# Four fused cross-attention blocks on one core: expert rows routed by scattered ids, the router's pairs placed in other slots, late rows centred on VectorE, input rows loaded by group

## The chip, the cores and the metric

The kernel runs on one core of one Trainium2 chip. The metric is the device time of one execution in microseconds (us); shown are the median and the range of several executions. The engines are called PE (TensorE, matmuls), DVE (VectorE), ACT (ScalarE), POOL (GpSimd) and SP (SyncE, which here only issues DMAs). "Landing" is the moment at which the last part of a DMA has arrived.

## What is computed

The input x has 16 sequences of 128 rows of width 256 (2,048 rows in all), and so has the context. Four layers follow one another. The first is the one that the change is in:

```python
q = _ln(latents, ...); x = latents + _mha(q, q, ...)        # self-attention, 16 heads of 16
x = x + _mha(_ln(x, ...), _ln(tokens, ...), ...)            # cross-attention
h = _ln(x, moe_ln_g, moe_ln_b)
logits = h @ rw.T + rb                                      # 8 experts
vals, idx = jax.lax.top_k(logits, 2)
gates = jax.nn.softmax(vals, axis=-1)
h1 = gelu(h @ fc1_w[e].T + fc1_b[e])                        # width 1024, each expert e
eo = h1 @ fc2_w[e].T + fc2_b[e]
x = x + (eo[idx] * gates).sum(axis=1)                       # the two chosen experts of each row
```

Then come a layer that picks the 10 best rows of each sequence and lets them attend to the context, a grouped-query attention with a gated feed-forward part, and a last cross-attention with ternary weights. All arithmetic is in fp32.

## The kernel before

The program is a row of blocks; at the end of each (`end_turn`, L231) all engines meet and the semaphores are cleared.

**Constants and first loads** (L274 to L307) are a block of their own: SP loads all of x (2 MB) and the weights of the self-attention, ACT issues eight small loads, POOL writes the constants.

**`attention`** (L517) runs self- and cross-attention as one stream of 32 sequences, t = 0 to 31, in slots; what each engine does in slot t is written out by hand, engine by engine, so the order on each is fixed. Four sequences form a group whose rows are centred on POOL (L898), turned on PE (L629), projected (L636, L645). Each slot then has scores for the row maxima (PE L653, DVE L943), turned scores (PE L663), exponentials (ACT L873), products (PE L673, L678), division (DVE L964) and, for two sequences together, the output rows (PE L688). VP and xn_a are views of the large tile `reg`.

**The router** (class `Router`, L1052) works inside the last slots of that stream, by tables of slots. Rows go in pairs of sequences q = 0 to 7: statistics (DVE L1072, L1075), the deviation (POOL L1080, L1081), centring (POOL L1083), turning (PE L1090), gain and bias (ACT L1096), logits (PE L1104). Sets of sequences k are then ranked and chosen (DVE L1123 to L1137), counted (PE L1148, L1149) and placed (DVE L1154 to L1164): every row gets for each of its two experts a row number in `expert_rows`, a scratch tensor in DRAM of 17,280 rows of 1 KB, which 36 DMAs of SP fill with zeros beforehand (L316). POOL scatters the rows there, one indirect DMA for each sequence and choice, 32 in all (L1177). At the end DVE makes the tables of which expert each of 39 blocks of 128 rows belongs to (L1184 to L1201), and the gates (L1214 to L1224). Where the jobs of PE share a bank of PSUM, the lists `in_a`, `in_b`, `in_c` give their order in the bank.

**The experts' block** takes 39 blocks j = 0 to 38: SP reads 128 rows (`load_rows`, L1044), 1 MB of first weights (`load_up`, L1034) and 1 MB of second weights (`load_down`, L1039) per block into two buffers each, and stores the result over the same rows (`store_rows`, L1049). PE turns the rows (L1289), makes 16 matmuls 128x128 (L1300) and 8 matmuls 128x256 (L1310), each in two passes. SP issues these in this order for j:

```python
sp.wait_ge(M["turned_in"], j + 1); load_rows(sp, j + 2)
sp.wait_ge(M["fc1_full"], FC * (j + 1)); load_up(sp, j + 2)
sp.wait_ge(M["fc2_full"], j); load_down(sp, j + 1)
sp.wait_ge(M["y_ok"], j); store_rows(sp, j - 1)
```

**The next block** collects the results: POOL gathers both expert rows of each sequence (L1457, 32 indirect DMAs), DVE adds them times their gates (`take`, L1733), scores and ranks rows (L1741 to L1771); meanwhile PE projects the context (L1472 to L1490). DVE clears the padded values tok_V first (L1819) and then adds the bias row (L1821), whose bank PE needs next. SP waits for the first gathers and loads the mask and the six weights of the third layer (L323), which POOL scales afterwards (L1463).

## Time and profile before

| | |
|---|---|
| median of 3 runs | 1471.12 us (1466.84 to 1472.11) |
| the profiled execution's own time | 1468.97 us |
| its span, first to last instruction | 1467.2 us |
| PE busy | 1292.2 us (88%) |
| DVE busy | 673.1 us (46%) |
| ACT busy | 621.1 us (42%) |
| POOL busy | 398.9 us (27%) |
| bytes moved by DMA | 139.67 MB |

Busy times are sums over the whole span. The span and the time differ by 1.8 us that lie outside the first and last instruction. In rows of the timeline the first number is the start, the second the duration, both in us; "x4" is the number of instructions merged into the row; in square brackets stands how long the engine had been idle before it and what ended that.

### The profile page before, as it was taken

The page shows a single profiled execution, that of the slowest core. Times are in us where ns is not written, and L with a number is a line of the kernel's source. Part 1 is how long each engine was busy: PE and PEld are TensorE (multiplying, and loading weights), DVE is VectorE, ACT ScalarE, POOL GpSimd, SP SyncE. Part 2 cuts the span into 40 slices and gives each one's busy share as a digit, 9 for nine tenths or more (in the row PEclk, how much of TensorE's full clock was granted, in tenths as well). Part 3 has the DMA queues.
Part 4 walks back from the last instruction along what each step waited for, and adds up shares of the span by engine and source line. Part 5 has one row for each costly group of instructions (what it writes and reads, how often), then busy time and mean ns, then how long its engine had stood idle before and what let it go on. Part 6 is the DMA issues. An engine that isn't in the chain of part 4 may idle for free. (4 is left out here: it accounts for less than half of the span.)

```text
span 1467.2 us, 34284 instructions
## 1 busy us (share of the span) xinstructions
PE 1292.2 (88%) x13938; PEld 1054.0 (72%) x13938; DVE 673.1 (46%) x1410; ACT 621.1 (42%) x1444; POOL 398.9 (27%) x517
## 2 busy tenths in 40 slices
PE   3899999973499999997888569999999999878997
PEld 1566666663489999995576458888888888655665
DVE  3576777784231000003473356455454453336666
ACT  1444445430244444452412036556455564324442
POOL 5224445156000000002640044424334242142200
PEclk9999999996699999998956789999999999989999
DMA  9900000011589999993700000000000000000000
GB/s 352 414 6 2 2 2 2 2 41 61 200 279 330 324 326 330 326 331 122 266 2 2 2 2 1 2 2 1 1 1 2 2 1 1 1 1 2 17 16 30
DMA packets 83324, 139.67 MB, mean 95 GB/s; under 512 B 5344, under 2 KB 63712, under 8 KB 83040
## 3 DMA queue, kind: packets, MB, share of 16 engines
q1 hardware_dynamic: 78816, 128.07, 24.9%
q0 software_dynamic: 3072, 8.39, 1.6%
q8 instruction: 112, 1.84, 0.5%
q10 hardware_dynamic: 1280, 1.01, 0.2%
q14 instruction: 44, 0.36, 0.1%
HBM read 108.36 MB, written 29.10 MB: 94 GB/s over the span
## 5 line engine op out<-in xcount | busy, mean ns | idle before, releaser
L1344 ACT ACTIVATE w_ca<-scores,fc1b 128x128 f32<-128x128 f32 x312 | 113.7, 367 | 139.6 <-PE scores L1300 119.7
L873 ACT ACTIVATE reg<-scores 128x1024 f32<-128x1024 f32 x96 | 93.0, 1021 | 143.6 <-PE scores L663 143.2
L1300 PEld LDWEIGHTS scores<-reg 128*128 128x128 f32 x1248 | 148.1, 195 | 4.5 <-issue 2.6
L1300 PE MATMUL scores<-reg 128*128 128x128 f32 x1248 | 148.6, 278 | 2.1 <-issue 1.1
L943 DVE TENSOR_REDUCE reg<-scores 128x8 f32<-128x1024 f32 x96 | 113.0, 1219 | 63.0 <-PE scores L653 63.0
L1310 PE MATMUL bank<-reg,w_ca 128*128 128x256 f32 x624 | 141.1, 379 | 0.3 <-DVE small L1358 0.3
L2042 ACT ACTIVATE reg<-reg,mx 128x128 f32<-128x128 f32 x256 | 99.2, 389 | 83.8 <-DVE mx L2222 83.5
L1367 DVE TENSOR_TENSOR reg<-bank,reg 128x256 f32<-128x256 f32 x39 | 16.6, 425 | 240.8 <-PE bank L1310 228.5
L1310 PEld LDWEIGHTS bank<-reg,w_ca 128*128 128x128 f32 x624 | 115.5, 190 | 14.6 <-DVE small L1358 0.3
L2131 POOL TENSOR_TENSOR reg<-reg,rden 128x512 f32<-128x512 f32 x64 | 66.5, 1040 | 210.8 <-DVE rden L2227 210.7
L1958 PE MATMUL scores<-reg 128*128 128x128 f32 x1024 | 122.4, 279 | 0.5 <-ACT reg L2065 0.5
L1958 PEld LDWEIGHTS scores<-reg 128*128 128x128 f32 x1024 | 119.7, 196 | 0.7 <-ACT reg L2065 0.7
L1951 PE MATMUL bank<-reg 128*128 128x256 f32 x512 | 118.8, 385 | 0.8 <-issue 0.8
L1457 POOL DMA_INDIRECT reg<-expert_rows,pick_row x32 | 30.7, 958 | 326.5 <-issue 320.4
L1951 PEld LDWEIGHTS bank<-reg 128*128 128x128 f32 x512 | 94.7, 190 | 26.6 <-issue 13.2
L964 DVE RECIPROCAL reg<-bank 128x256 f32<-128x256 f32 x48 | 84.2, 1754 | 31.9 <-PE bank L678 30.9
L820 ACT ACTIVATE reg<-bank,qk_bias,shape_c 128x512 f32<-128x512 f32 x96 | 69.5, 778 | 56.4 <-PE bank L636 56.0
L1958 PE MATMUL bank<-reg 128*128 128x128 f32 x640 | 78.4, 279 | 0.7 <-ACT reg L2072 0.7
L1958 PEld LDWEIGHTS bank<-reg 128*128 128x128 f32 x640 | 76.7, 195 | 1.9 <-ACT reg L2072 1.1
L2249 DVE TENSOR_TENSOR reg<-scores,reg 128x512 f32<-128x512 f32 x32 | 22.1, 692 | 109.8 <-PE scores L1958 109.8
L653 PEld LDWEIGHTS scores<-reg 32*128 32x128 f32 x1536 | 48.7, 190 | 28.1 <-ACT reg L873 22.9
L663 PEld LDWEIGHTS scores<-reg 32*128 32x128 f32 x1536 | 47.5, 186 | 25.1 <-issue 25.0
(258 smaller groups left out, 2283.3 us busy)
## 6 DMA issues: line engine op xcount, KB each, us to landing
reg<-in_fc SPq DMA_DIRECT2D x78, 1024.0 KB, 7.5
expert_rows<-reg SPq DMA_DIRECT2D x36, 480.0 KB, 14.7
reg<-expert_rows SPq DMA_DIRECT2D x39, 128.0 KB, 5.9
expert_rows<-reg SPq DMA_DIRECT2D x39, 128.0 KB, 6.8
xres<-in_x SPq DMA_DIRECT2D x1, 2048.0 KB, 11.4
ctxr<-in_ctx SPq DMA_DIRECT2D x1, 2048.0 KB, 8.2
w_l<-in_w_l SPq DMA_DIRECT2D x2, 1024.0 KB, 11.8
out<-xres SPq DMA_DIRECT2D x8, 256.0 KB, 2.7
```

The lines of the kernel that those rows point to most:

```text
L653: ins = nc.tensor.matmul(S[r][:, (2 * s + c) * P:(2 * s + c + 1) * P], Qs[rows_of(r), (b // GB) % 2, s, c, batch(b)], Ks[rows_of(r), (b // ...
L820: ins = nc.scalar.activation(dst[:, g % 2, s, m, :], bank[:, :], ACT.Identity, scale=scale[:, s:s + 1], bias=bias[:, s, m:m + 1])
L873: ins = nc.scalar.activation(PT2[:, t % 2, 2 * half:2 * half + 2, :, :, :].rearrange("p r s c q -> p (r s c q)"), scores4[:, 2 * half:2 * ...
L943: ins = nc.vector.tensor_reduce(mxpad.rearrange("p (c n d) -> p n c d", c=C, d=DH)[:, 4 * half:4 * half + 4, :, 0], scores4[:, 2 * half:2 ...
L964: link(nc.vector.reciprocal(rd, banks[4][:, 2 * P:4 * P]))
L1300: ins = nc.tensor.matmul(S[n % 4][:, 0:P], up_w8[j % 2][:, c, f * P:(f + 1) * P], xbT[:, j % 2, c, :], start=(c == 0), stop=(c == C - 1))
L1310: ins = nc.tensor.matmul(T[j % 2][:, 0:D], h1[:, j % 2, f, :], down_w8[j % 2][:, f, :], start=(f == 0), stop=(f == FC - 1))
L1344: nc.scalar.activation(h1[:, j % 2, f, :], S[n % 4][:, 0:P], ACT.Gelu, bias=fc1b[:, bass.ds(e * FC + f, 1)]).then_inc(M["fc1_free"], 1)
L1951: ins = nc.tensor.matmul(bank[:, 0:D], src[:, f, :], w[:, f, :], start=(f == 0), stop=(f == FC - 1))
L1958: ins = nc.tensor.matmul(bank[:, k * P:(k + 1) * P], w[:, c, w0:w0 + P], src[:, c, :], start=(c == 0), stop=(c == C - 1))
L2042: ins = nc.scalar.activation(v[:, a, :], v[:, a, :], ACT.Exp, bias=cols_of(mx, n)[:, a:a + 1], accum_out=cols_of(psum, n)[:, a:a + 1])
L2131: nc.gpsimd.tensor_tensor(v, v, spread(rden, n), ALU.mult).then_inc(M["scaled"], 1)
```

## The change

It has these parts.

- **Routing by ids.** The rows no longer travel. The centred rows are stored once, pair by pair, as `routed_rows` (`store_routed`, SP). POOL scatters for each row and choice only two int32 numbers, the row's own number and the number of its result row, into `sorted_ids`, which nine DMAs fill with padding ids beforehand in place of the 36 DMAs of zeros. In the experts' block SP loads the 128 id pairs of a block four blocks ahead (`load_ids`), POOL gathers the rows by the first id (`gather_rows`) and scatters the results by the second into `expert_out` (`scatter_rows`), where both results of a row lie side by side. The next block reads them with 16 plain DMAs on SP (`expert_rows_in`), instead of 32 gathers on POOL.
- **Slots.** The router's first pairs are turned and ranked two slots sooner, in seven sets instead of five. From slot 27 (`LATE`) on, the router's jobs stand behind the attention's on PE, ACT and DVE.
- **Late rows on DVE.** Pairs 5 to 7 are centred on DVE; POOL only makes the deviations (`late_rstd`).
- **Rows by group.** The first block is gone; its work stands at the head of `attention`. x is loaded in four DMAs, one per group, and the first group is centred on DVE.
- **Weights.** Five of the six weights of the third layer are loaded among the experts' blocks (`grouped_at`). Of the experts' first weights, only one block's goes out before the ids are there.
- **The rest.** The gates are finished in the experts' block; POOL clears tok_V, in three parts.

```diff
+        id_dram = nc.dram_tensor("sorted_ids", (SROWS, 2), mybir.dt.int32, kind="Internal").ap()
+        xn_dram = nc.dram_tensor("routed_rows", (B * P, D), F32, kind="Internal").ap()
+        ys_dram = nc.dram_tensor("expert_out", (YROWS, D), F32, kind="Internal").ap()
...
-        ZEROS = 36
-        ZN = SROWS * D // P // ZEROS
...
-        zeros = view(17408, [ZN])
...
-                sp.dma_start(xres[:], A["x"].rearrange("b p d -> p b d")).then_inc(ld["x"], 16)
...
-        end_turn()
...
+        def first_rows(sp):
+
+            for g in range(G):
+                sp.dma_start(xres[:, g * GB:(g + 1) * GB, :], A["x"].rearrange("b p d -> p b d")[:, g * GB:(g + 1) * GB, :])\
+                    .then_inc(ld_x[g], 16)
+                if g == 0:
+                    sp.dma_start(w_sa[:], A["w_sa"].rearrange("(c p) n -> p c n", p=P)).then_inc(ld["sa"], 16)
...
-            for k in range(ZEROS):
-                sp.dma_start(xs_dram.rearrange("(p r) d -> p (r d)", p=P)[:, k * ZN:(k + 1) * ZN], zeros)\
-                    .then_inc(ld["zeros"], 16)
+            sp.wait_ge(M["ids_ok"], 1)
+            for a in range(ID_PARTS):
+                sp.dma_start(id_dram[a * P * ID_ROWS:(a + 1) * P * ID_ROWS, :].rearrange("(p r) d -> p (r d)", p=P),
+                             padding_ids[:, :, :].rearrange("p r d -> p (r d)")).then_inc(ld["ids"], 16)
             sp.dma_start(down_bias, A["fc2b"]).then_inc(ld["fc2b"], 16)
...
+        def store_routed(sp, q):
+
+            sp.wait_ge(M["rows_ok"], 2 * q + 2)
+            sp.dma_start(xn_dram.rearrange("(b p) d -> p b d", p=P)[:, 2 * q:2 * q + 2, :], routed[:, 2 * q:2 * q + 2, :])\
+                .then_inc(ld["xn"], 16)
...
-                    in_c.append(("y", pair_out(t)))
+                    (in_c if router is None or t < LATE else in_b).append(("y", pair_out(t)))
+                if t >= LATE:
+                    turns = [("rx", q) for q in routed("turn", t)]
+                    results = [("re", t)] if has_results(t) else []
+                    in_c += results + turns if t < N + 1 else turns + results
...
+                        if t < LATE:
+                            routed_turns(t)
+                            routed_results(t)
...
+                        if LATE <= t < N + 1:
+                            routed_results(t)
+                            routed_turns(t)
+                        if t >= N + 1:
+                            routed_turns(t)
+                            routed_results(t)
...
-                                pool.wait_ge(ld["zeros"], 16 * ZEROS)
+                            if g == 0:
+                                pool.sem_inc(M["rstd_ok"], 1)
+                                continue
...
-                            router.centre(pool, link, q)
+                            if q < router.ON_VECTOR:
+                                router.centre(pool, nc.gpsimd, link, q)
+                            elif q + 1 < B // 2:
+                                router.late_rstd(pool, link, q)
+                        if router is not None and t + 1 == router.slots["stats"][-1]:
+                            router.late_rstd(pool, link, B // 2 - 1)
                         for k in routed_sets("place", t):
                             router.scatter(pool, k)
                     if router is not None:
-                        pool.wait_ge(M["scattered"], 16 * 2 * B)
+                        pool.wait_ge(ld["xn"], 16 * B // 2)
+                        gather_rows(pool, 0)
+                        gather_rows(pool, 1)
...
+                            dve.wait_ge(M["rstd_ok"], 1)
+                            for j in range(GB):
+                                nc.vector.tensor_scalar(xn_a[:, j, :], xres[:, j, :], mv[:, 0, j, 0:1], rstd[:, 0, j:j + 1],
+                                                        ALU.subtract, ALU.mult).then_inc(M["hx_ok"], 1)
                             nc.vector.memset(mxpad, 0.0)
-                            nc.vector.memset(VP[:, :, :, :, :], 0.0).then_inc(M["pad_ok"], 1)
+                            nc.vector.memset(VP[:, 0, :, :, :], 0.0).then_inc(M["pad_ok"], 1)
+                            nc.vector.memset(VP[:, 1, :, :, :], 0.0).then_inc(M["pad_ok"], 1)
...
+                            if q >= router.ON_VECTOR:
+                                router.centre(dve, nc.vector, link, q)
+                        if t >= LATE:
+                            take_results(t)
...
+        def load_ids(sp, j):
 
             r = sp.value_load(block_row[0:1, j:j + 1], min_val=0, max_val=SROWS - P)
-            sp.dma_start(xb[:, j % 2, :], xs_dram[bass.ds(r, P), :]).then_inc(rows_in[j % 2], 16)
-
-        def store_rows(sp, j):
-
-            r = sp.value_load(block_row[0:1, j:j + 1], min_val=0, max_val=SROWS - P)
-            sp.dma_start(ys_dram[bass.ds(r, P), :], yb[:, j % 2, :]).then_inc(y_stored[j % 2], 16)
+            sp.dma_start(block_ids_of[:, j, :], id_dram[bass.ds(r, P), :]).then_inc(ids_in[j % 4], 16)
+
+        def gather_rows(pool, j):
+
+            pool.wait_ge(ids_in[j % 4], 16 * (j // 4 + 1))
+            if j >= 2:
+                pool.wait_ge(M["turned_in"], j - 1)
+            nc.gpsimd.indirect_dma_start(xb[:, j % 2, :], None, xn_dram,
+                                         bass.IndirectOffsetOnAxis(block_ids_of[:, j, 0:1], 0)).then_inc(rows_in[j % 2], 16)
+
+        def scatter_rows(pool, j):
+
+            pool.wait_ge(M["y_ok"], j + 1)
+            if j >= 1:
+                pool.wait_ge(y_stored[(j - 1) % 2], 16 * ((j - 1) // 2 + 1))
+            nc.gpsimd.indirect_dma_start(ys_dram, bass.IndirectOffsetOnAxis(block_ids_of[:, j, 1:2], 0),
+                                         yb[:, j % 2, :], None).then_inc(y_stored[j % 2], 16)
...
-                "turn": [23, 24, 25, 27, 29, 31, 33, 35],
-                "logits": [26, 26, 28, 28, 32, 32, 34, 36],
+                "turn": [22, 23, 25, 27, 29, 31, 33, 35],
+                "logits": [24, 24, 26, 28, 30, 32, 34, 36],
             }
 
-            sets = [(0, 4), (4, 4), (8, 4), (12, 2), (14, 2)]
+            sets = [(0, 4), (4, 2), (6, 2), (8, 2), (10, 2), (12, 2), (14, 2)]
             set_slots = {
-                "rank": [26, 28, 32, 34, 36],
-                "choose": [27, 29, 32, 34, 36],
-                "count": [28, 30, 33, 35, 37],
-                "place": [28, 30, 33, 35, 37],
+                "rank": [24, 26, 28, 30, 32, 34, 36],
+                "choose": [25, 26, 28, 30, 32, 34, 36],
+                "count": [26, 27, 29, 31, 33, 35, 37],
+                "place": [26, 27, 29, 31, 33, 35, 37],
             }
+
+            ON_VECTOR = 5
...
+            def late_rstd(self, pool, link, q):
+                self.deviations(pool, link, q)
+                pool.sem_inc(M["late_rstd"], 1)
+
+            def centre(self, eng, ops, link, q):
+                if q < self.ON_VECTOR:
+                    self.deviations(eng, link, q)
+                else:
+                    eng.wait_ge(M["late_rstd"], q - self.ON_VECTOR + 1)
...
-                        nc.gpsimd.indirect_dma_start(xs_dram, bass.IndirectOffsetOnAxis(pick_row[:, s, b:b + 1], 0),
-                                                     routed[:, b, :], None).then_inc(M["scattered"], 16)
+                        nc.gpsimd.indirect_dma_start(id_dram, bass.IndirectOffsetOnAxis(pick_row[:, s, b:b + 1], 0),
+                                                     token_ids[:, b, s, :], None).then_inc(M["scattered"], 16)
...
-                    load_up(sp, j)
-                    load_down(sp, j)
+                load_up(sp, 0)
                 sp.wait_ge(M["tables"], 2)
                 sp.wait_ge(M["scattered"], 16 * 2 * B)
-                for j in range(2):
-                    load_rows(sp, j)
+                for j in range(4):
+                    load_ids(sp, j)
+                load_up(sp, 1)
...
+        grouped_at = {8: "wkv2", 13: "wo2", 18: "wg2", 23: "wu2", 28: "wd2"}
...
-                        load_rows(sp, j + 2)
+                        if j + 4 < NBLK:
+                            load_ids(sp, j + 4)
                         sp.wait_ge(M["fc1_full"], FC * (j + 1))
                         load_up(sp, j + 2)
-                    if j >= 1:
-                        if j + 1 < NBLK:
-                            sp.wait_ge(M["fc2_full"], j)
-                            load_down(sp, j + 1)
-                        sp.wait_ge(M["y_ok"], j)
-                        store_rows(sp, j - 1)
+                    if j >= 1 and j + 1 < NBLK:
+                        sp.wait_ge(M["fc2_full"], j)
+                        load_down(sp, j + 1)
+                    if j in grouped_at:
+                        load_grouped(sp, grouped_at[j])
...
+                for j in range(NBLK):
+                    if j + 2 < NBLK:
+                        gather_rows(pool, j + 2)
+                    if j >= 2:
+                        scatter_rows(pool, j - 2)
+                scatter_rows(pool, NBLK - 2)
+                scatter_rows(pool, NBLK - 1)
...
+                def expert_rows_in(g):
+                    if g >= 2:
+                        sp.wait_ge(M["taken"], 2 * GB * (g - 1))
+                    for j in range(GB):
+                        b = g * GB + j
+                        sp.dma_start(picked[:, g % 2, j, :, :].rearrange("p k d -> p (k d)"),
+                                     ys_dram[2 * P * b:2 * P * (b + 1), :].rearrange("(p k) d -> p (k d)", k=2))\
+                            .then_inc(ld_pick[b], 16)
...
-                            nc.gpsimd.indirect_dma_start(picked[:, g % 2, j, k, :], None, ys_dram,
-                                                         bass.IndirectOffsetOnAxis(pick_row[:, k, g * GB + j:g * GB + j + 1], 0))\
-                                .then_inc(ld_pick[g * GB + j], 16)
+                for k in range(3):
+                    nc.gpsimd.memset(tok_V[:, k, :, :, :], 0.0).then_inc(M["pad_ok"], 1)
...
-                nc.vector.memset(tok_V[:, :, :, :, :], 0.0).then_inc(M["pad_ok"], 1)
```

How the order moves is shown at three places. The first is DVE at the start of the program, before:

```order
L928 BN_STATS st<-xres 128x6
L933 BN_AGGR mv<-st 128x2
L989 TENSOR_SCALAR reg<-ones,cols 128x128 x2
...
L995 TENSOR_SCALAR qk_bias<-cols,shape_c 128x2
L997 MEMSET reg 128x256
L998 MEMSET reg 128x4096
L1000 TENSOR_TENSOR route<-bank,rows 128x256
```

and in the change:

```order
L1056 TENSOR_SCALAR reg<-ones,cols 128x128 x2
...
L1062 TENSOR_SCALAR qk_bias<-cols,shape_c 128x2
L1066 TENSOR_SCALAR reg<-xres,mv,rstd 128x256 x4
L1068 MEMSET reg 128x256
L1069 MEMSET reg 128x2048
L1070 MEMSET reg 128x2048
L1072 CAST padding_ids<-shape_c 128x30
L1074 CAST token_ids<-shape_c 128x64
L1077 TENSOR_TENSOR route<-bank,rows 128x256
```

The first group's centring (L1066) has come to DVE, ahead of the clearing of VP (`reg`), which is in two halves; POOL no longer does it.

The second is PE in slots 31 to 34. L663 (now L687) are the turned scores of the last sequence, L673 and L678 (L697, L702) its products, L688 (L712) output rows, L1090 (L1198) turns a pair for the router, L1104 (L1212) makes logits, L1148 and L1149 (L1256, L1257) count. Before:

```order
L1090 MATMUL bank<-ident,reg 128x128 x4
L663 MATMUL scores<-reg 128x128 x16
L688 MATMUL bank<-w_ca,reg 128x256 x4
L673 MATMUL bank<-reg 32x128 x16
L678 MATMUL bank<-reg,ones_half 32x256 x8
L1104 MATMUL bank<-rw,reg 128x8 x8
L1090 MATMUL bank<-ident,reg 128x128 x4
L1148 MATMUL bank<-w_sa 128x32
L1149 MATMUL bank<-w_sa,ones 128x32
L688 MATMUL bank<-w_ca,reg 128x256 x4
```

and in the change:

```order
L687 MATMUL scores<-reg 128x128 x16
L712 MATMUL bank<-w_ca,reg 128x256 x4
L1256 MATMUL bank<-w_sa 128x16
L1257 MATMUL bank<-w_sa,ones 128x16
L1198 MATMUL bank<-ident,reg 128x128 x4
L697 MATMUL bank<-reg 32x128 x16
L702 MATMUL bank<-reg,ones_half 32x256 x8
L1212 MATMUL bank<-rw,reg 128x8 x4
L712 MATMUL bank<-w_ca,reg 128x256 x4
L1198 MATMUL bank<-ident,reg 128x128 x4
```

The turning of a pair no longer stands ahead of the turned scores or of the last output rows.

The third is POOL in the router's last slots. L1080 and L1081 (now L1178, L1179) make the deviation, L1083 (L1191) centres two sequences, L1177 (L1286) are the scatters. Before:

```order
L1083 TENSOR_SCALAR reg<-xres,small 128x256 x2
L1177 DMA expert_rows<-reg,pick_row 17280x256 x8
L1080 TENSOR_SCALAR small<-small 128x2
L1081 TENSOR_TENSOR small<-small,nhalf 128x2
L1083 TENSOR_SCALAR reg<-xres,small 128x256 x2
L1177 DMA expert_rows<-reg,pick_row 17280x256 x8
```

and in the change:

```order
L1286 DMA sorted_ids<-token_ids,pick_row 17280x2 x4
L1178 TENSOR_SCALAR small<-small 128x2
L1179 TENSOR_TENSOR small<-small,nhalf 128x2
L1178 TENSOR_SCALAR small<-small 128x2
L1179 TENSOR_TENSOR small<-small,nhalf 128x2
L1286 DMA sorted_ids<-token_ids,pick_row 17280x2 x12
L1136 DMA reg<-routed_rows,block_ids_of 128x256 x2
```

The centring of the late pairs is gone from POOL, both last deviations stand ahead of the last twelve scatters, and the first two gathers of rows (L1136) stand behind them in the same block.

## Rows read from the trace of the kernel before

**Rows 1.** Busy time by stretch, all engines: experts' blocks, and the block after them
```profile
core 0: us, PE busy (x) PEld busy (x) DVE busy (x) ACT busy (x) POOL busy (x), PEclk, DMA share, GB/s
...
450.00:700.00 250.00, 239.01 (x1587) 220.44 (x1587) 27.18 (x63) 115.56 (x315) 13.44 (x14) 0.97 0.88 296
...
710.00:720.00 10.00, 7.85 (x38) 5.06 (x37) 8.40 (x38) 2.47 (x5) 3.03 (x4) 0.84 1.02 399
```

**Rows 2.** Timeline of the start: ACT's last small load, DVE, POOL, PE
```profile
4.20 0.56 ACTq L290 DMA_DIRECT2D rw<-in_rw  x1
...
15.39 0.45 DVE L989 TENSOR_SCALAR reg<-ones,cols 128x128 f32<-128x128 f32 x2
...
17.03 4.90 POOL L898 TENSOR_SCALAR reg<-xres,mv,rstd 128x256 f32<-128x256 f32 x4
...
17.66 0.27 DVE L997 MEMSET reg<- 128x256 f32 x1
...
21.99 1.97 PE L629 MATMUL bank<-ident,reg 128*128 128x128 f32 x8 [3.96 <-POOL reg L898]
```

**Rows 3.** DMA issues by line: queue, count, KB each, median us from issue to landing
```profile
reg<-in_fc SPq DMA_DIRECT2D x78, 1024.0 KB, 7.5
...
expert_rows<-reg,pick_row POOLq DMA_INDIRECT x32, 2.4
reg<-expert_rows,pick_row POOLq DMA_INDIRECT x32, 3.7
...
rw<-in_rw ACTq DMA_DIRECT2D x1, 8.0 KB, 7.7
```

**Rows 4.** Timeline of slots 31 and 32: PE turning a pair, last turned scores, last division
```profile
325.41 0.63 PE L1090 MATMUL bank<-ident,reg 128*128 128x128 f32 x4 [3.02 <-POOL reg L1083]
...
325.97 1.17 PE L663 MATMUL scores<-reg 32*128 32x128 f32 x32
...
331.21 1.76 DVE L964 RECIPROCAL reg<-bank 128x256 f32<-128x256 f32 x1 [1.34 <-PE bank L678]
```

**Rows 5.** Timeline of the router's last pairs: DVE, POOL and PE
```profile
346.08 0.74 DVE L1072 BATCH_NORM_STATS2 small<-xres 128x6 f32<-128x256 f32 x2
...
353.57 0.73 POOL L1081 TENSOR_TENSOR small<-small,nhalf 128x2 f32<-128x2 f32 x1
...
356.98 1.09 PE L1090 MATMUL bank<-ident,reg 128*128 128x128 f32 x4 [11.03 <-POOL reg L1083]
...
361.43 0.29 DVE L1123 TENSOR_TENSOR w_sa<-w_sa 128x128 f32<-128x128 f32 x1
...
363.31 0.37 DVE L1137 TENSOR_TENSOR w_sa<-w_sa 128x8 f32<-128x8 f32 x2
...
366.18 0.17 DVE L1164 CAST pick_row<-w_sa 128x2 int32<-128x2 f32 x1
```

**Rows 6.** Timeline from the last scatters to the experts' first turn
```profile
370.41 0.96 POOL L1177 DMA_INDIRECT expert_rows<-reg,pick_row  x1 [0.30 <-issue]
...
377.38 1.47 SPq L1044 DMA_DIRECT2D reg<-expert_rows  x2
...
382.85 2.46 DVE L1355 TENSOR_REDUCE small<-w_l 128x1 f32<-128x512 f32 x4 [8.57 <-PEq L231]
...
385.01 0.69 PE L1289 MATMUL bank<-ident,reg 128*128 128x128 f32 x2 [19.76 <-DMA reg<-expert_rows]
```

**Rows 7.** Timeline of two experts' blocks: PE's first matmuls of each
```profile
659.04 3.73 PE L1300 MATMUL scores<-reg 128*128 128x128 f32 x32
...
666.29 3.73 PE L1300 MATMUL scores<-reg 128*128 128x128 f32 x32
```

**Rows 8.** Timeline of the two blocks after the experts: DVE, PE
```profile
684.53 5.18 DVE L1819 MEMSET reg<- 128x6144 f32 x1 [1.23 <-issue]
...
690.04 1.11 PE L1472 MATMUL bank<-ident,ctxr 128*128 128x128 f32 x4 [4.61 <-DVE route L1821]
...
847.23 0.35 DVE L2196 TENSOR_SCALAR reg<-xres,rstd 128x256 f32<-128x256 f32 x1 [1.68 <-POOL rstd L2125]
```

230 lines of the change are left out of this document (131 added, 99 removed).

## The prediction

> **What bounds the kernel now.** I read the busy time by stretch first. PE is busy for 239 of 250 us among the experts and DMA is then busy for 0.88 of the time [rows 1], so there the matmuls set the pace, with DMA close behind. The change touches that stretch little; what it can win lies at three places where PE stands still, which the timeline shows.
>
> At the start PE turns its first rows at 21.99 us, and had waited 3.96 us for POOL's centring [rows 2]. At the end of the router it waits for POOL three times: 3.02 us at 325.41 [rows 4] and 11.03 us at 356.98 [rows 5] are two of them. POOL spends 0.96 us on each indirect DMA and 0.30 between two [rows 6], so 32 of them take 40 us of the engine that must also centre the late pairs. Then comes the longest gap, 19.76 us until the experts' first rows land, PE starting at 385.01 [rows 6]. The third place is small: at 690.04 PE has waited 4.61 us for DVE's bias row, which stands behind a memset of 5.18 us [rows 8].
>
> **The start.** Today the statistics and the bias columns end at 17.93 (17.66 + 0.27, with the memset), 2.3 us after the bias columns begin at 15.39, and POOL centres from 17.03 for 4.90 us [rows 2]. In the change DVE needs a quarter of x, then the small loads, the last of which is asked for at 4.20 [rows 2] and landed 7.7 us later [rows 3], at 11.9. That load competes with the same megabytes of x and weights as before, so I leave it there. Bias columns to 14.2; then DVE centres, four times 0.35 us [rows 8], to 15.6 with the gaps; PE turns at 15.9. 21.99 less 15.9 is **6.1 us** won. It cannot be more than 10 (the meeting of the engines that is gone ends at about 13 us, the loads remain), and if x in four parts delays the small loads it may be 3. DVE's memset of VP now stands behind the centring, its statistics for group 1 come at about the same time as PE's work moves forward, and POOL has lost 4.9 us of centring, so I cost that at nothing. The 36 DMAs of zeros go; nobody waits for them in the rows, so they are worth nothing.
>
> **The last slots of attention.** Call T the start of the last turned scores, 325.97 today [rows 4]. The 3.02 us ahead of it [rows 4] go, since no turning stands before the turned scores any more. Against that, DVE, whose maxima and divisions lie in each slot's chain, gets more there: ranking and choosing a set of two took 361.43 to 363.68, 2.25 us [rows 5], and now comes in slots 26, 28 and 30 too, the first time beside a set of four's places; in slot 30 DVE also waits for POOL's deviation (0.73 us, [rows 5]) and centres (0.7). How much of it is hidden no row shows; between 0 and 8 us, I take 3, since a slot has room on DVE after its subtraction. The two cancel: **0**.
>
> **The tail.** DVE ends the last division at T + 7.0 (331.21 + 1.76, [rows 4]). Then it works in rounds: statistics 0.74 [rows 5], a wait for POOL's 0.73, centring 0.7, ranking and choosing 2.25, and with about 1 us for small operations and gaps that is 5.4 us; then counting on PE and placing, 363.68 to 366.35, 2.7 us [rows 5]. Two such rounds of 8.1 us, and a last one of 2.25 + 2.7 and 0.6 for the gates' first half: T + 29. POOL has sent the earlier sets by then (its last deviation is at about T + 18, the eight scatters before the last four take 10 us), so the last four start at T + 29.5, the last of them at 33.5, and it lands 2.4 us later [rows 3], at T + 36. SP then issues four loads of ids and one of weights. Two issues took 1.47 us with 0.35 for the second's own [rows 6], so 1.12 each, 5.6 in all: T + 42. The meeting of the engines cost 4.0 us (378.85 to 382.85, [rows 6]): T + 46. The gathered rows are there: ids at 36 + 1 + 2.4, gather 0.96 to issue and 3.7 to land [rows 3] is T + 44. PE starts at T + 46.5, where today it starts at 385.01, T + 59.0 [rows 6]. **12.5 us** won. No row prices a load of 8 bytes per partition; between 2.4 and 7.5 us [rows 3] I take 2.4, as it has hardly any bytes and no weights before it but one block's.
>
> **The experts.** PE's period is 7.25 us (659.04 to 666.29, [rows 7]). A block moves 2.36 MB, which is 325 GB/s. POOL now issues one gather and one scatter per block, 2.5 us of the 7.25, and each has a whole block to land. Row loads stay 128 KB. The new demand is 4.7 MB of the third layer's weights in blocks 8 to 28. One such load is about 3 us of DMA; a weight load lands 7.5 us after issue [rows 3] and is needed 10 us after it (two periods less one 3.73 us of matmuls [rows 7], less the issue), so one more megabyte just fits and must be worked off in five blocks: 5 times 2.36 plus 1.05 MB in 36.2 us, 355 GB/s. DMA has moved 399 GB/s at 710 us [rows 1]. I take **2 us** lost, between 0 and 12 (4.7 MB at 399 GB/s, nothing hidden). The Trainium skill, *DMA: Bandwidth & Descriptors*, section Bandwidth, has 341 GB/s for transfers of 1 MB; by it the 31 blocks from 8 on, 77.9 MB, would take 228.4 us instead of 224.6, and 3.8 us would be lost in place of 2. The trace speaks against it as a ceiling by the 399 just named.
>
> **After the experts.** The last store is an indirect DMA, issued in 0.96 us and landing in 2.4 like those of [rows 3], where SP's took about a microsecond less: 1 us lost. DVE's memset of 5.18 us [rows 8] goes to POOL, and PE's bank comes free 5 us sooner. POOL's scaling of weights now starts sooner, when DVE ranks the first rows for PE; how much it slows DVE no row shows, between 0 and the 5 us just won; I take 1.5. Together **2.5 us** won. The 32 gathers that go from POOL were not waited for by PE.
>
> **The sum.** 6.1 + 0 + 12.5 - 2 + 2.5 = 19.1 us. From the profiled execution's own time, 1468.97, that is 1449.9. It lies 2.15 us below the median of the runs, 1471.12, so the changed kernel's median may lie at 1449.9 to 1452.1; I say 1451.
>
> **The rivals.**
> *More is won.* DVE's added work in the slots is hidden wholly (3 more), the small loads land sooner with x behind them (3 more), no DMA waits (2), the scaling hurts nobody (1.5), and the experts' first blocks run without the waits that SP's long list brought: 1440. For it: SP no longer stands behind results. Against it: four things must go well together.
> *DVE becomes the bound.* In the last slots it centres, waits for POOL and ranks; 5 us more before T (8 in place of 3) and 2 us more in each of the rounds, since each wait for POOL can fall behind a scatter of 1.26 us: 10 us less won, 1461. For it: DVE then carries statistics, centring, ranks and places in one queue. Against it: it idled for most of the tail before.
> *The start gives nothing.* x by group does not do what it says, if the small loads behind it on the same DMA engines set the start: 1457.
> *Slower: DMA becomes the bound among the experts.* The gathers and scatters, with ids in 8-byte pieces and the added weights, make the blocks wait. The price is 39 times what a block gains in length. From 0.5 us per block on, all that is won is gone; at 0.72 it is 28 us lost, 1479. A block would then have 7.97 us for its 2.36 MB and 0.12 MB of added weights, 311 GB/s. For it: DMA is busy for 0.88 of the stretch already, and the part may be higher where no block waits. Against it: 399 GB/s in the stretch in which POOL's gathers and the same weights ran together [rows 1].
>
> **How the numbers follow.** The forecast 0.54, more 0.17, DVE 0.17, the start 0.06, DMA 0.06. The forecast's own range, from the bounds above, is 1443 to 1459. The range for 8 in 10 reaches to both middle rivals: 1436 to 1464. A difference of 0.5%, 7.4 us, is about what can be told from none. Faster than 1463.8: nearly all of the forecast, all of the first and third rival and two thirds of the second, 0.86. Slower than 1478.5: 0.05. Between: 0.09.
>
> **What would show it.** In the new profile PE's first turning should start near 16 us; the last turned scores near 320; the first turn among the experts near 366; the wait of PE for POOL's centring should be gone, and DVE busy from division to last place with waits for POOL of a microsecond. Among the experts the period should stay 7.25 us, with gaps of under a microsecond behind blocks 8, 13, 18, 23 and 28. The prediction is wrong in its main part if PE's first expert turn comes less than 8 us sooner after T than 59 us, and wrong in its sign only if the period grows.

## The result, and the profile after

The change is worth almost nothing where it was first compared. The kernel before took 1471.41 us (median of 20 runs, 1466.84 to 1473.22), the changed one 1467.66 us (20 runs, 1462.45 to 1472.35); the ratio is 0.9982, 95% interval 0.9974 to 0.999. That is faster by 2.6 us by the ratio (3.75 by the medians), where 20 were forecast, and 1467.66 lies outside the range of 1436 to 1464.

The experiments ran on other chips, and there the same two kernels differ by much more: 1503.2 us before (9 runs), 1481.5 after (5 runs), ratio 0.9855, interval 0.9834 to 0.9876. They were four chips, numbers 10, 4, 1 and 9; on each of them the kernel before has a median of 1501.0 to 1503.2 us, and below they are called "the later chips". (The expectations, written at the time, say "the second chip" for all four.) The number of the first comparison's chip is not known; it is "the first chip" here. Nothing is compared across the two kinds unless it is said.

The two profiled executions of the first chip, laid side by side (each moment is the start of an instruction that both kernels have; "lead" is by how much the changed kernel is ahead):

| moment | before | after | lead | step |
|---|---|---|---|---|
| PE turns the first rows | 21.99 | 16.91 | 5.1 | +5.1 |
| turned scores of slot 20 | 225.33 | 220.08 | 5.3 | +0.2 |
| last turned scores, T | 325.97 | 329.38 | -3.4 | **-8.7** |
| experts' first turn on PE | 385.01 | 388.13 | -3.1 | +0.3 |
| DVE's last bias of the experts | 677.71 | 680.43 | -2.7 | +0.4 |
| first DVE operation of the next block | 681.91 | 690.98 | -9.1 | **-6.4** |
| first of the third layer | 844.52 | 845.86 | -1.3 | **+7.7** |
| first of the last layer | 1297.54 | 1298.94 | -1.4 | -0.1 |
| end of the span | 1467.2 | 1465.5 | 1.7 | **+3.1** |

So the gain was not absent: 16.8 us were won in six steps and 15.2 given back in three. The rows behind the table follow, from the timeline of the changed kernel (columns as in the rows of before). The start, which answers to [rows 2]:

```profile
4.65 0.46 ACTq L303 DMA_DIRECT2D rw<-in_rw  x1
...
13.40 0.48 DVE L1056 TENSOR_SCALAR reg<-ones,cols 128x128 f32<-128x128 f32 x2 [6.02 <-DMA rw<-in_rw]
...
15.47 1.38 DVE L1066 TENSOR_SCALAR reg<-xres,mv,rstd 128x256 f32<-128x256 f32 x4
...
16.91 1.97 PE L653 MATMUL bank<-ident,reg 128*128 128x128 f32 x8 [0.83 <-DVE reg L1066]
```

DVE waits for the last small load to 13.40, centres in 1.38, and PE turns at 16.91. Slot 22, where the lead of 5.3 us begins to go:

```profile
243.15 0.63 PE L1198 MATMUL bank<-ident,reg 128*128 128x128 f32 x4 [2.92 <-POOL reg L1191]
243.71 2.09 PE L687 MATMUL scores<-reg 32*128 32x128 f32 x32
```

The first pair is turned one slot sooner than before, ahead of the turned scores of slot 22, and POOL has not centred it: PE waits 2.92 us, and after the wait the 32 matmuls take 2.09 us instead of 1.17. PE's granted clock, as a share of the full 2.4 GHz, is 0.62 from 243 to 246 us, a mean of its two levels 1.2 and 2.4 GHz; before the wait it was 1.0. (The list of the change says that the first pairs are turned two slots sooner; it is one slot for the turning and two for the ranking.) Before the change, the turned scores of this slot came 10.05 us behind those of slot 21; now 13.6. By the turned scores of slot 24 the changed kernel has lost 6.3 us (42.4 us from slot 20 against 36.1). The turned scores of slots 27 and 28, and what follows them:

```profile
293.98 1.26 PE L687 MATMUL scores<-reg 32*128 32x128 f32 x32 [3.37 <-DVE reg L1012]
...
303.91 1.17 PE L687 MATMUL scores<-reg 32*128 32x128 f32 x32 [0.77 <-DVE reg L1012]
...
308.90 1.94 ACT L919 ACTIVATE reg<-scores 128x1024 f32<-128x1024 f32 x2 [7.68 <-remote]
308.95 0.87 DVE L1044 SCALAR_TENSOR_TENSOR reg<-bank,shape_c,reg 128x256 f32<-128x256 f32 x2 [2.47 <-remote]
310.89 1.45 PE L677 MATMUL scores<-reg 32*128 32x128 f32 x20 [4.65 <-ACT reg L919]
```

At 293.98, in slot 27, PE waits for DVE's maxima, which stand behind the places of one set and the ranks of the next. At 308.9 two engines wake together from a wait that no instruction of the trace ends ("remote"): the scores they wait for are marked as done at 305.1. No run isolates this one gap; the experiments show gaps of its kind on the later chips. The tail, with the last division, DVE's last place, the first weight load, the last scatter, SP's loads of ids, the second gather and PE's first turn among the experts, which answer to [rows 5, 6]:

```profile
339.47 1.76 DVE L1033 RECIPROCAL reg<-bank 128x256 f32<-128x256 f32 x1 [2.34 <-PE bank L702]
...
363.51 0.17 DVE L1272 CAST pick_row<-w_sa 128x2 int32<-128x2 f32 x1
...
367.56 0.40 SPq L1119 DMA_DIRECT2D reg<-in_fc  x1
...
367.74 0.96 POOL L1286 DMA_INDIRECT sorted_ids<-token_ids,pick_row  x1 [0.30 <-issue]
...
376.01 3.68 SPq L1129 DMA_DIRECT2D block_ids_of<-sorted_ids  x4
...
380.14 0.97 POOL L1136 DMA_INDIRECT reg<-routed_rows,block_ids_of  x1 [0.30 <-issue]
...
388.13 0.66 PE L1400 MATMUL bank<-ident,reg 128*128 128x128 f32 x2 [25.03 <-PEq L245]
```

Eight us lie between the last scatter and SP's answer, and another seven between the second gather and the end of the meeting. What the meeting holds is seen by its own line (columns: duration in ns min/median/max, first and last start), at 381 and at 684 us, and, in the kernel before, at 379 us:

```profile
L245 POOLq DRAIN  x1: 6022/6022/6022, 381.3 to 381.3; - x1
...
L245 POOLq DRAIN  x1: 6257/6257/6257, 683.9 to 683.9; - x1
```

```profile
L231 POOLq DRAIN  x1: 2678/2678/2678, 379.3 to 379.3; - x1
```

POOL does not meet the others before its drain is over. After the experts it costs 6.26 us that the kernel before did not have. The experts themselves went as forecast (period 7.24 us, 661.41 to 668.65), in answer to [rows 1, 7]:

```profile
450.00:700.00 250.00, 234.16 (x1578) 218.20 (x1577) 22.32 (x52) 113.18 (x310) 64.77 (x64) 0.97 0.92 318
...
661.41 3.73 PE L1411 MATMUL scores<-reg 128*128 128x128 f32 x32
...
668.65 3.73 PE L1411 MATMUL scores<-reg 128*128 128x128 f32 x32
```

And the block after them, in answer to [rows 8], and the last layer:

```profile
690.94 5.48 POOL L1582 MEMSET reg<- 128x2048 f32 x3 [8.85 <-POOLq L245]
690.98 1.91 DVE L1934 TENSOR_SCALAR reg<-ones,cols 128x128 f32<-128x128 f32 x2 [10.13 <-PEq L245]
...
694.87 1.92 PE L1595 MATMUL bank<-ident,ctxr 128*128 128x128 f32 x8
...
1302.64 1.38 DVE L1066 TENSOR_SCALAR reg<-xres,mv,rstd 128x256 f32<-128x256 f32 x4 [0.46 <-POOLq L946]
...
1304.07 1.67 PE L653 MATMUL bank<-ident,reg 128*128 128x128 f32 x8 [0.54 <-DVE reg L1066]
```

PE's wait of 4.61 us for the bias row is gone (context rows turned at 694.87, 3.9 us behind DVE's start instead of 8.1). The last layer's attention also has its first group centred on DVE: its first turning comes 5.1 us after its first statistics, 8.6 before.

### The profile page after: what moved, and what is told of

It is laid out like the page before. It is cut to its first block and busy times, and to the rows that moved or that the text cites. A ratio compares the mean times of both kernels' runs of the same rounds, so it can differ in the third digit from the quotient of the medians.

```text
span 1465.5 us, 34213 instructions
## 1 busy us (share of the span) xinstructions
PE 1293.6 (88%) x13946; PEld 1057.4 (72%) x13946; DVE 677.2 (46%) x1457; ACT 621.7 (42%) x1444; POOL 431.4 (29%) x551
## 5 line engine op out<-in xcount | busy, mean ns | idle before, releaser
L1421 PEld LDWEIGHTS bank<-reg,w_ca 128*128 128x128 f32 x624 | 115.9, 191 | 14.2 <-DVE small L1476 0.3
L1144 POOL DMA_INDIRECT expert_out<-reg,block_ids_of x39 | 38.7, 992 | 153.1 <-DVE reg L1485 96.6
L687 PEld LDWEIGHTS scores<-reg 32*128 32x128 f32 x1536 | 48.5, 190 | 28.7 <-issue 28.7
## 6 DMA issues: line engine op xcount, KB each, us to landing
ctxr<-in_ctx SPq DMA_DIRECT2D x1, 2048.0 KB, 15.2
```

The source lines that it names most:

```text
L1421: ins = nc.tensor.matmul(T[j % 2][:, 0:D], h1[:, j % 2, f, :], down_w8[j % 2][:, f, :], start=(f == 0), stop=(f == FC - 1))
```

## The experiments

All ran on the later chips. Two things must be known to read them. The changed kernel itself ran on chips 10 and 4 only, so the ratio to the kernel before, which ran on each of the four, compares better than the medians do. And executions of one kernel there differ by 3.3 to 3.7 us already before the router begins (in the changed kernel and its variants slot 20's turned scores start at 216.1 to 216.9, or at 219.6 to 221.2), where PE's granted clock dips in slots 1 and 10 or does not. So beside the medians I give three distances from the profiled executions: slot 20 to T, T to the experts' first turn, and their sum. While scatters run in the slots, a single profile leaves some 4 us open in the first of these: the edit of the late first weights lies behind T, and yet it has 123.9, where three other profiles whose edits lie behind T or that have none show 119.5 to 120.0.

| kernel | chip | median us | ratio to before | 20 to T | T to experts | sum |
|---|---|---|---|---|---|---|
| before | all | 1501.0 to 1503.2 | | 108.0 | 63.5 | 171.5 |
| changed | 10 | 1481.5 | 0.9855 | 120.0 | 58.4 | 178.4 |
| changed, again | 4 | 1477.8 | 0.9844 | 120.0 | 58.2 | 178.2 |
| drains among the experts | 1 | 1473.5 | 0.9819 | 119.5 | 58.6 | 178.0 |
| first weights late | 1 | 1476.3 | 0.9828 | 123.9 | 55.1 | 179.0 |
| first pairs turned in slot 23, 24 | 1 | 1476.2 | 0.9828 | 120.0 | 58.9 | 178.9 |
| old slot tables | 1 | 1475.5 | 0.9831 | 105.9 | 69.3 | 175.2 |
| ids in rows of 64 bytes | 10 | 1472.5 | 0.9809 | 119.0 | 56.3 | 175.3 |
| late pairs centred on POOL | 4 | 1478.8 | 0.9849 | 118.1 | 62.6 | 180.7 |
| scatters held back | 4 | 1489.5 | 0.9931 | 109.5 | 83.1 | 192.6 |

On the first chip the sums are 159.7 before and 168.1 after (100.6 + 59.0, 109.3 + 58.8).

**Both kernels on later chips.** No edit; both ran on chip 10, the changed one again on chip 4.

> The changed kernel itself, beside the others on their chip, since the four experiments before showed the kernel before 30 us slower (1501) than in the first comparison, and themselves at 1474 to 1476. Theory 'stutter': while POOL scatters pieces of 8 bytes, PE waits in its own queue (gaps of 0.3 to 1.5 us between single matmuls that wait for no semaphore) and a 16 KB packet of instructions takes 2 to 3.4 us instead of at most 1.5; this differs from chip to chip, so T (the last turned scores) will lie anywhere from 329 to 344 and the time follows it. Rival: the experiments' own edits caused it; then T is 329 here too.

> The kernel before with a profile, on the chip of the others. If this chip is one that makes the kernel before slow (1501), the profile shows where; theory: not in the slots (T within 2 us of 326, its scatters are of 1 KB pieces) but among the experts, where 1 KB scattered rows and the loads share the DMA engines, or in the wait for the scatters. If it is a chip like the first, 1467 to 1473.

> The changed kernel once more, beside the next three, since the chip decides much: 1467.7 on the first, 1481.5 on the second. On the second chip I expect 1480 to 1483, T (last turned scores) at 338 to 341, PE's first turn among the experts at 398 to 399; on a chip like the first 1467 and 329.

Measured: 1481.53 us (1477.88 to 1486.06) and 1477.84 (1476.93 to 1479.09) for the changed kernel, T at 340.2 and 336.5; 1500.97 for the one before, T at 334.4. I had expected the kernel before to be disturbed among the experts and not in the slots. It is the other way round: from the first turn among the experts to the last it has 275.8 us, and 277.7 on the first chip. But slots 29 and 30 (from the turned scores of each to the next) have 14.2 and 8.9 us instead of 7.0 and 8.8, and the block after the experts 182.1 us instead of 162.6. There PE stands still with no semaphore to wait for while POOL issues its 32 gathers. The timeline of the kernel before on chip 10, PE:

```profile
713.79 0.66 PE L1472 MATMUL bank<-ident,ctxr 128*128 128x128 f32 x4 [1.26 <-issue]
727.10 1.12 PE L1472 MATMUL bank<-ident,ctxr 128*128 128x128 f32 x4 [12.64 <-issue]
```

The changed kernel has no indirect DMA in that block, and there it has 157.3 us on chip 10 (159.3 on chip 4, 154.9 on the first chip). This is why the change is worth 22 us on chip 10 and 3 on the first: 24.8 us against 7.7 in this one block. That the gathers alone do it there is not shown: during the wait of 12.64 us weights of the third layer are being loaded too (DMA moves 408 GB/s from 714 to 727.5 us), and five of these loads have also left the block with the change. In the slots, its scatters of ids do to PE what the scatters of rows did; the timeline of PE in slot 28, changed kernel, chip 10:

```profile
303.24 0.29 PE L697 MATMUL bank<-reg 128*32 128x128 f32 x1 [0.45 <-issue]
303.95 0.27 PE L697 MATMUL bank<-reg 128*32 128x128 f32 x1 [0.42 <-issue]
304.67 0.40 PE L697 MATMUL bank<-reg 128*32 128x128 f32 x3 [0.45 <-issue]
306.08 0.65 PE L697 MATMUL bank<-reg 128*32 128x128 f32 x3 [1.01 <-issue]
```

32 matmuls that take 1.08 us in other slots are spread over 7 us, one or a few at a time.

**Scatters held back.** None of POOL's scatters runs beside slots 26 to 32.

```diff
-                        for k in routed_sets("place", t):
-                            router.scatter(pool, k)
+                        if router is not None and t >= 33:
+                            for k in (range(5) if t == 33 else routed_sets("place", t)):
+                                router.scatter(pool, k)
```

> All scatters of ids of the first five sets are held back to slot 33, so that none runs while the attention's slots 26 to 32 do. Theory 'stutter': PE's gaps that wait for no semaphore come from POOL's indirect DMAs beside it; without them T lies 100 to 106 us behind slot 20's turned scores (108.0 in the kernel before and 119.9 in the changed one on the second chip), so T at 320 to 326 and slots 28 to 31 at 8 to 10 us each; the 20 scatters then take 25 us behind T and PE's first turn comes at T + 66 to 70, so the time falls by 2 to 8 on the second chip and is the same or worse on the first. Rival 'DVE': slots 27 to 31 are long because DVE ranks and centres there; T stays within 3 us of the changed kernel's and the time rises by 9.

Measured: 1489.46 us (1487.0 to 1496.99), where I had expected it to fall by 2 to 8. From slot 20 to T 109.5 us instead of 120.0 on the same chip, which is the first chip's 109.3, though not the 100 to 106 that I expected. The waits of PE from 260 to 345 us (us in total, times, longest), changed kernel on chip 10:

```profile
PE scores L687 <- DVE reg L1012: 3.9, 2, 3.4
PE bank L697 <- issue: 3.7, 7, 1.0
...
PE scores L677 <- issue: 1.7, 1, 1.7
PE scores L687 <- issue: 0.9, 1, 0.9
```

and with the scatters held back, where no wait of PE is left that ends on "issue":

```profile
PE scores L687 <- DVE reg L1013: 8.0, 4, 3.4
PE bank L1199 <- DVE w_sa L1263: 2.2, 3, 1.7
```

So the stutter in the slots, single matmuls some tenths of a microsecond apart with no semaphore to wait for, comes from POOL's indirect DMAs: that is shown. It also shows that the 8.7 us which the first chip lost before T do not need the stutter: with none, the distance is the same 109.5. The waits for DVE's maxima, 8.0 us, remain: DVE's ranking and placing in the slots' chain. That the held-back version is slower was to be had from the rows of before: 20 scatters of 1.26 us now stand one after another on POOL, and the tail grows by all of their 25 us, not by the 8 to 12 that my T + 66 to 70 allowed.

**The first pairs turned one slot later.**

```diff
-                "turn": [22, 23, 25, 27, 29, 31, 33, 35],
-                "logits": [24, 24, 26, 28, 30, 32, 34, 36],
+                "turn": [23, 24, 25, 27, 29, 31, 33, 35],
+                "logits": [25, 25, 26, 28, 30, 32, 34, 36],
...
-                "rank": [24, 26, 28, 30, 32, 34, 36],
+                "rank": [25, 26, 28, 30, 32, 34, 36],
```

> The first two pairs are turned in slots 23 and 24 (as before the change), their logits made and ranked in slot 25. Theory 'early turn': PE's wait of 2.92 us for POOL's centring in slot 22, and the half clock that follows it, go; the turned scores of slot 22 start at 240.2 instead of 243.7 and those of slot 31 at about 325 instead of 329.4; the time falls by 3 to 5 us. Rival 'moved': DVE's ranking of four sequences now stands in slot 25 beside the subtraction there and the slots after it lose what was won; T stays at 328 to 330 and the time does not move.

Measured: 1476.16 us (1471.45 to 1478.46). The timeline of PE in slots 22 and 23:

```profile
240.53 1.17 PE L687 MATMUL scores<-reg 32*128 32x128 f32 x32
...
247.91 0.60 PE L1198 MATMUL bank<-ident,reg 128*128 128x128 f32 x4
248.44 1.17 PE L687 MATMUL scores<-reg 32*128 32x128 f32 x32
```

The wait and the fallen clock are gone, and at slot 24 the kernel is 6.3 us ahead of the changed one (36.1 us from slot 20 against 42.4). Slot 25, with the ranking of four sequences, takes 3.1 back, and by T nothing is left that could be told (120.0). The first theory holds for its slot, the rival for the sum, as long as the scatters run in the slots; without them it is otherwise, as the variants at the end show.

**Old slot tables,** in all else the changed kernel (the tables and the five sets as before the change, shown in the diff above).

> All slot tables and the five sets as before the change, the rest of the change kept (late jobs behind the attention's, late pairs centred on DVE, ids). Theory 'slots cost': the last turned scores start at 320 to 323 instead of 329.4, as seven sets put ranking and choosing into more slots' chains; but the larger sets 8 to 11 are ranked in slot 32 and lengthen the tail by 2 to 4 us; the time falls by 3 to 6. Rival 'LATE and DVE': the delay of slots 27 to 31 comes from the order from slot 27 on and DVE's centring, and stays with the old tables; T at 325 or more and the time within 2 us of the changed kernel.

Measured: 1475.49 us (1471.63 to 1478.87). T comes 14 us sooner (105.9 from slot 20 against 120.0), more than I expected, and the tail takes 10.9 of it back (69.3 against 58.4). The new tables (earlier turning, seven sets), then, buy 11 us behind T and pay 14 ahead of it. The order from slot 27 on and the centring on DVE are not what delays T: they are in this kernel too, and it has 2.1 us less than the kernel before (108.0).

**Late pairs centred on POOL.**

```diff
-            ON_VECTOR = 5
+            ON_VECTOR = 8
...
-                        if router is not None and t + 1 == router.slots["stats"][-1]:
-                            router.late_rstd(pool, link, B // 2 - 1)
```

> All pairs are centred on POOL again (only this part undone). Theory: centring on DVE is worth its place in the tail, where each of the last rounds waits for it: POOL's centring of a pair takes 2.4 us against 0.74, so two rounds grow by 1.7 us each, and a centring that falls behind four scatters waits 5 us more; T loses or wins at most 1, PE's first turn at T + 62 to 68 instead of T + 58.6, the time 3 to 8 us more. Rival: DVE's load in the slots is what delays T; then T falls by 3 or more and the time is the same or lower.

Measured: 1478.8 us (1476.35 to 1482.91), the sum of distances 180.7 against 178.2 on the same chip: the tail 4.4 us longer, T 1.9 sooner. By the distances, centring on DVE is worth 2.5 us, less than the 12.5 of the tail that I had put on it and the order together; the medians, 1478.8 and 1477.84, do not tell the two apart, where 3 to 8 us had been expected.

**The first weight load behind the loads of ids.**

```diff
-                load_up(sp, 0)
                 sp.wait_ge(M["tables"], 2)
                 sp.wait_ge(M["scattered"], 16 * 2 * B)
                 for j in range(4):
                     load_ids(sp, j)
+                load_up(sp, 0)
                 load_up(sp, 1)
```

> The experts' first weight load goes behind the loads of ids instead of ahead of the wait for the scatters. Theory 'queue': the last scatter landed 7.7 us after its issue began because the megabyte of weights was in the same DMA engines ahead of it; it now lands after 2.4, SP loads the ids 4 to 5 us sooner, and PE's first turn among the experts comes 3 to 4.5 us sooner (388.1 to 384.5 or so); the time falls by 3 to 4. Rival 'small writes': scatters of 8 bytes are slow by themselves at the end of a run of 12; nothing moves, or PE starts later by up to 3 us, as the weights now land last.

**Ids in rows of 64 bytes.** `sorted_ids` has 16 numbers in a row instead of two; a scatter writes 64 bytes, the loads still read the first two.

```diff
+IDW = 16
...
-        id_dram = nc.dram_tensor("sorted_ids", (SROWS, 2), mybir.dt.int32, kind="Internal").ap()
+        id_dram = nc.dram_tensor("sorted_ids", (SROWS, IDW), mybir.dt.int32, kind="Internal").ap()
...
-                                                     token_ids[:, b, s, :], None)
+                                                     token_flat[:, 4 * b + 2 * s:4 * b + 2 * s + IDW], None)
```

> The id table's rows are widened from 8 to 64 bytes, so each scatter writes 128 pieces of 64 bytes (what follows the ids in a row is never read). Theory 'small pieces': writes of 8 bytes are served slower than they come and pile up in DRAM, which delays their landing (to 7 us and more) and the fetching of instructions; with 64 bytes a scatter lands after 2.4 us, no instruction packet takes over 1.5 us in slots 26 to 37, T comes to 318 to 323, SP's loads of ids follow the last scatter by 3 to 4 us, and the time is 8 to 15 us below the changed kernel beside it. Rival 'pieces count': it is the number of pieces (128 per DMA, one DMA each 1.26 us), whatever their size; then T and the landing stay as in the changed kernel and the time is the same within 2 us. The padding's nine DMAs carry 1.1 MB instead of 0.14 early in the program; I expect nothing from that.

Measured: first weights late 1476.33 us (1472.39 to 1478.03), wide ids 1472.47 (1470.65 to 1476.19). The wide ids are 9.1 us below the changed kernel on the same chip by the medians; the sum of distances has 3.1 of it, and 3.4 lie ahead of slot 20 (216.83 against 220.22), where the edit does nothing. The stutter hardly cares about the size: 119.0 us from slot 20 to T, where 318 to 323 for T itself was forecast and 335.8 came, so the rival holds there. But between the start of the last scatter and SP's first load of ids, a wait that is the landing alone, both edits act, and they add up (the lower row is of kernels described below, which differ in more):

| | 8 bytes | 64 bytes |
|---|---|---|
| weight load ahead | 8.45 (378.05 to 386.50) | 5.79 (373.83 to 379.62) |
| weight load behind | 5.33 (375.35 to 380.68) | 3.16 (370.95 to 374.11) |

With the weight load moved and nothing else the wait is 5.59 us (381.78 to 387.37), against 8.27 to 9.03 in the three profiles of the changed kernel. So the megabyte ahead or beside costs 2.6 to 3.1 us, the small pieces 2.2 to 2.7 with twelve scatters in a row. With all 32 in a row and no megabyte in flight the pieces cost more: 7.81 us with 8 bytes (394.00 to 401.81, scatters held back) and 3.16 with 64 (384.55 to 387.71, the first of the variants at the end). Scatters of 8 bytes are slow by themselves, then, and the more so the more of them run together, as the rival of the moved weight load had it; both theories hold in part. The Trainium skill, *DMA: Bandwidth & Descriptors*, section Queues, rings and completion order, says that the write which reports a DMA as done lands only after all earlier writes of its DMA engine, across its queues; a load issued on SP's queue ahead of POOL's last scatter then holds the scatter's report back. The upper row fits this; that the scatter's pieces themselves stand behind the megabyte would give the same times, and no run separates the two. The same page, section Specifications, puts the size below which a DMA engine reads, changes and writes back at 512 bytes; 8 and 64 bytes lie both below it and yet differ by 2 us and more here, so that rule alone does not explain the second effect.

**Drains among the experts.**

```diff
                     if j >= 2:
                         scatter_rows(pool, j - 2)
+                    if j % 6 == 5:
+                        nc.gpsimd.drain()
```

> POOL's DRAIN ahead of the meeting of the engines took 6.26 us after the experts (76 indirect DMAs issued since the last one), though the last scatter had landed; before the change it took 2.68 us in the block with 32 scatters and 2.66 in the one with 32 gathers. Theory 'count': a drain costs 0.083 us for each indirect DMA issued since the last drain. A drain every six blocks among the experts then leaves some 6 for the last: it takes about 0.5 us, the block ends 5.5 us sooner, the time falls by 5 to 6 us, and each early drain takes about 1 us in POOL's idle time. Rival 'landing': the drain waits for the last transfers' completion, whatever their number; the last one stays at 6 us and the time does not move. Second rival: the early drains hold the gathers up and PE waits for rows; the experts' stretch grows by some us.

Measured: 1473.51 us (1472.66 to 1475.17). The last drain:

```profile
L245 POOLq DRAIN  x1: 537/537/537, 693.4 to 693.4; - x1
```

From PE's last turn among the experts to the clearing of the semaphores there are 19.5 us, and 25.2 in the changed kernel: 5.7 won, as forecast. The changed kernel was not run on this chip; the ratios to the kernel before, 0.9819 against 0.9855 and 0.9844, fit with intervals that overlap. A drain costs 6.257 us for 76 indirect DMAs, 2.678 and 2.661 for 32, 0.537 for 6: 0.082 to 0.090 us each, and all nine profiles with 76 show 6.257. A drain with none costs 0.04. Wrong was the price of the early ones: 6 to 8 us each, not 1; transfers are in flight at each of them, and the drain seems to wait for these. POOL had the time; the experts' stretch is 277.0 us, against 278.2 and 275.0 in the two profiles of the changed kernel on later chips.

**A version that beats both.** Wide ids, the first pairs turned in slots 23 and 24, drains every six blocks and behind two sets of scatters, the first weights behind the ids and the second in the experts' block.

```diff
                         for k in routed_sets("place", t):
                             router.scatter(pool, k)
+                            if k in (2, 3):
+                                nc.gpsimd.drain()
...
-                load_up(sp, 0)
                 sp.wait_ge(M["tables"], 2)
                 sp.wait_ge(M["scattered"], 16 * 2 * B)
                 for j in range(4):
                     load_ids(sp, j)
-                load_up(sp, 1)
+                load_up(sp, 0)
...
                 load_down(sp, 0)
+                load_up(sp, 1)
                 load_down(sp, 1)
```

> Wide ids as in the kernel beside it, the first two pairs turned in slots 23 and 24, drains of POOL every six blocks and after two sets of scatters, and the first weight load behind the loads of ids, the second in the next block. Theory: the causes add up: against the kernel with wide ids alone 5.5 us from the last drain, 3 to 5 from the slots, 2 to 4 from the gap ahead of the experts: 11 to 14 us less. PE's first turn comes at T + 48 to 52. Rival: the gap ahead of the experts is set by the landing of the gathers in any order, and only 8 us are won.

> The wide version once more, to stand beside the other two on one chip: 1457 to 1461 on the second chip, 1445 to 1452 if the chip is like the first.

Measured: 1459.05 us (1456.31 to 1463.49), ratio to the kernel before 0.9718, interval 0.97 to 0.9735; the second time 1463.67 (1458.95 to 1467.0), 0.9742, interval 0.9721 to 0.9762. The first is 22.5 us below the changed kernel on the same chip, and 13.4 below the wide ids alone, as forecast (11 to 14); the second, on chip 9, is 14 to 18 us below the changed kernel's two medians and misses its own forecast of 1457 to 1461. Its sums are 165.6 and 166.7, with PE's first turn at T + 50.4 and T + 50.6, as the last scatter is seen after 3.16 us and the drain is short. The two drains between the scatters took 7.0 and 6.4 us of POOL each. The meeting ahead of the experts, gather, drain and first turn:

```profile
374.11 3.73 SPq L1135 DMA_DIRECT2D block_ids_of<-sorted_ids  x4
376.50 1.00 POOL L1142 DMA_INDIRECT reg<-routed_rows,block_ids_of  x1 [4.59 <-DMA block_ids_of<-sorted_ids]
...
382.24 0.66 PE L1408 MATMUL bank<-ident,reg 128*128 128x128 f32 x2 [15.93 <-PEq L247]
```

```profile
L247 POOLq DRAIN  x1: 1973/1973/1973, 379.4 to 379.4; - x1
```

It was not run on the first chip, so that it beats both there is an inference and not shown: what it removes (5.7 us of drain after the experts, some 8 of the gap ahead of them) is in the first chip's profile too.

**Variants of it.** With the scatters held back instead of the drains between them; with 8-byte ids; with 8-byte ids and the early pairs in two sets of four. The edit of the last:

```diff
-            sets = [(0, 4), (4, 2), (6, 2), (8, 2), (10, 2), (12, 2), (14, 2)]
+            sets = [(0, 4), (4, 4), (8, 2), (10, 2), (12, 2), (14, 2)]
...
-                "place": [26, 27, 29, 31, 33, 35, 37],
+                "place": [28, 30, 31, 33, 35, 37],
```

> The version that beat both (1459 on the second chip), but with the scatters held back to slot 33 instead of drains between them. Theory: T falls by 8 to 12 (no stutter), the tail grows by 8 to 10 and POOL's drain before the meeting of the engines is 2.8 us instead of 2.0; the time is within 4 us of 1459. Rival: the held scatters also delay the last ones beyond POOL's free time, and it is 5 to 10 us slower than 1459.

> The version that took 1459 on the second chip, with the id table back at 8 bytes a row. Rival 'pieces count' (the size of the pieces is nothing): the time is within 3 us of the wide version beside it, PE's gaps without a semaphore in slots 26 to 32 are 5 to 8 us in both. Theory 'small pieces': 4 to 8 us slower than the wide one, scatters land later, and SP's loads of ids follow the last scatter by 5 us or more in place of 3.2.

> 8-byte ids and everything else of the best version, but the early pairs in two sets of four as before the change (slots 26 to 30), the later ones in twos. Theory: T lay 105.9 us behind slot 20 with the old tables and 115.2 with seven sets, of which ranking in slots 24 to 28 has 3 to 5; so T is 3 to 6 us sooner than in the kernel with seven sets beside it, the tail the same (T + 50), the time 3 to 6 us less. Rival: sets of four rank for 2.7 us at a stretch and their eight scatters run together, so that the stutter is the same and T moves by under 2 us.

Measured: 1478.96 us (1476.58 to 1483.83), sum 183.5; 1467.84 (1466.62 to 1471.68), sum 172.5; 1467.25 (1465.46 to 1470.7), sum 169.8. Holding scatters back loses again, by its own length on POOL (T to experts 78.6), where a tie had been expected. The wide ids are worth 4 us by the medians of runs made together (1463.67 against 1467.84), as forecast, and 5.8 by the sums, 2.4 of it ahead of T (116.2 against 118.6, within what a single profile leaves open) and 3.4 behind. The six sets bring T 11.4 us nearer to slot 20 and give 8.7 of it back in the tail; the medians do not tell them apart, where 3 to 6 us had been expected.

The first of these variants also answers what the early turning costs. This variant and the kernel with the scatters held back ran on the same chip, neither has a scatter before T, and ahead of T they differ only in the slots of the first pairs (and in the width of an id table that nothing reads there). From slot 20 to T they have 104.9 us with the pairs turned in slots 23 and 24, and 109.5 with them in 22 and 23. So the early turning costs 4.5 us by T; in the experiment above, the stutter had covered this up. The 104.9 stand 4.3 us above the first chip's 100.6 before the change, which is what the seven sets, the new order and DVE's centring cost together without stutter.

## Why the prediction was wrong

Two steps of the prediction failed in the main: the landing of the last scatter and the meeting of the engines, in the term of the tail, and the zero for the last slots. The profiled span became 1.7 us shorter where 19.1 were forecast. The missing 17.4 are 12.2 in the tail, 8.7 in the slots, 1.1 after the experts and 1.0 at the start, less 2.4 that the experts did better, 3.1 of the last layer and 0.1 in small steps. The range did not follow from its terms either: the bounds given for the terms (3 to 10 us at the start, 0 to 8 in the slots, 2.4 to 7.5 for the landing, 0 to 12 among the experts, 0 to 5 for the scaling) reach, taken together, from 1440 to 1477 us, and not from 1443 to 1459; the 1467.66 lie within them.

**The start, 6.1 us: right.** 5.1. The small loads landed 1.5 us later than taken (DVE goes on at 13.40, forecast 11.9), the rest as worked out. The rival by which it gives nothing is out.

**The last slots, 0: wrong, the second largest error.** They lost 8.7 us. I took the loss of PE's wait (3.0) against 3 us of DVE's work, and named slots 26 to 30. The first 3.6 went in slot 22, and 6.3 were gone by slot 24, a place I had not looked at: the row of the order that moved there, a turning ahead of the turned scores, was in the diff ("turn": 23 to 22), and POOL's centring of the pair ended at about the time when PE came to it. The rule that I applied to the late pairs, who is late when a step is moved, was not applied to the early one. Then come DVE's rankings (3.37 us at slot 27), and one gap of 3.8 us with no semaphore, which adds nothing by T: without stutter the distance is 109.5 too. By the runs without stutter, 4.5 of the 8.7 us are the early turning, and about 4.3 the rest of the new tables, the order and DVE's centring; this goes across chips and was not run on the first. On the later chips, with stutter, the old tables were 14 us better ahead of T.

**The tail, 12.5 us: wrong, the largest error.** 0.3. The rounds on DVE were right: from the end of the last division to the last place 22.5 us against 22 forecast, the last scatter 4.2 us later against 4.5. But the last division ended at T + 11.9, not T + 7.0: a set's ranks and places now stand ahead of it on DVE, and PE's granted clock is 0.86 from 328 to 340 us and 0.73 from there to 346 (32 matmuls of L697 take 1.90 us at 335.81, 1.08 in other slots). The scatter was seen by SP 8.3 us after its issue began and not 2.5: I had priced its landing by a median of the scatters of before (2.4), and the change made its pieces 8 bytes and has a megabyte of weights ahead of it. [rows 6] warned of it: before the change, too, with four such loads issued by SP about the last scatter, SP's first load of rows came 7.0 us after that scatter's start (370.41 to 377.38). And the meeting took 7.3 us from SP's last issue instead of 4.0: POOL's drain takes 6.02 us instead of 2.68, behind the gathers that the change has placed ahead of it. By the price per DMA found above, 34 indirect DMAs make 2.8 of these; the other 3.2 end at about 384.5, when the second gather has landed if it took the 4.4 us that the view of its tile gives as the longest. That the drain waits for it is worked out, not shown by a run of its own. 4.9, 5.8 and 3.3 us, less 0.8 for SP's issues (4.8 us where I had 5.6) and 1 in small terms, are the 12.2 that are missing.

**The experts, 2 us lost: right within its range.** 0.4 won, period 7.24; a single wait of 1.33 us for the added weights, at 509.11. The slower rival, DMA as the bound, is out; DMA was busy for 0.92 of the time and moved 318 GB/s over the stretch.

**After the experts, 2.5 us: 1.4 won, out of larger parts that I did not see.** The last store was to cost 1 us and cost 6.4, by the drain. The memset's move gave 4.2 at PE, not 5: while POOL clears tok_V, two DVE operations that take 0.48 us at the start take 1.91 (DVE L1934), and the rest of the bias columns likewise. The Trainium skill, *SBUF — State Buffer*, section SBUF: two separate sides, has it that one pair of ports is shared by DVE, in its modes that use two ports, and POOL, and is held for a whole instruction, the other being blocked. The rows show the blocking; in which mode DVE ran they do not show. Since no indirect DMA is left in the block, its own drain of 2.66 us is gone as well, which I had not put in the sum.

**The last layer, 3.1 us won: not in the prediction at all.** The first group's centring is in `attention`, and a second layer calls it.

The rival "DVE becomes the bound" had the right mechanism for some 4 of the missing us before T and none for the early turning, the landing and the drain, so that it stopped at 1461.

## What to carry to other kernels

A step moved to an earlier slot has to be followed on every queue it passes and for its supplier as well: ask of the first one moved, not only of the last. Price a landing in the company that the change gives it (what is issued ahead of it, on any queue, how small its pieces are and how many like it run before it), and look in the rows for the same wait before taking a median, and count the drain of POOL in each meeting of the engines, by the number of indirect DMAs since the last one. When one kernel takes 1471 us in one place and 1501 in another, a forecast and its test belong on the same chip. An edit that seems to be worth nothing can be covered up by another wait behind it: undoing the early turning gave nothing with the stutter and 4.5 us by T without it.

## What the runs showed of the hardware

- **A drain of POOL costs 0.082 to 0.090 us for each indirect DMA since the last drain,** and not by whether they have landed: 2.68 us for 32, 6.26 for 76, 0.54 for 6. Behind transfers in flight it is longer (6.02 us for 34, 6 to 8 in the midst of the experts), which looks like waiting for them.
- **Scatters of 8 bytes a piece are slow to be seen as landed:** 7.8 us behind 32 in a row, 5.2 to 5.6 behind 12, against 3.2 with 64 bytes in both cases, with no load of weights in flight.
- **Indirect DMAs of POOL hold up PE's own stream.** In the slots no semaphore is waited for, DMA engines are nearly idle (3 GB/s from 302 to 310 us on chip 10), and single matmuls come 0.3 to 1 us apart. On the later chips this takes 10.5 us of the changed kernel's slots (with scatters 120.0 from slot 20 to T, without 109.5). It depends little on the size of the pieces, 8 or 64 bytes (120.0 and 119.0, 118.6 and 116.2). The wait of 12.64 us behind the experts looks alike, but there the DMA engines were busy with weights. What is held up was not shown. One guess, that it is the fetching of instructions, finds little support in the view of DMA queues (queue: packets, MB, share of 16 engines). On the first chip, between 310 and 315 us, the changed kernel and the one before:

```profile
q8 instruction: 1, 0.02, 3.0%
```

```profile
q0 software_dynamic: 191, 0.52, 26.0%
q8 instruction: 1, 0.02, 1.6%
```

One packet of instructions took 3.0% of 16 x 5 us, 2.4 us, and 1.3 us in the kernel before. But no scatter runs in that stretch of the changed kernel, and where PE stutters most, on chip 10 between 302 and 310 us, the packet took 1.1% of 16 x 8 us, 1.4 us:

```profile
q0 software_dynamic: 160, 0.01, 1.7%
q8 instruction: 1, 0.02, 1.1%
```

- **One kernel takes 1471 us in the first comparison and 1501 to 1503 on four later chips.** That it is the chip that makes the difference is likely and not shown, and how, stays open.
- **A wait of 2.92 us on PE cost more than itself:** the 32 matmuls behind it took 2.09 us instead of 1.17, at a mean granted clock of 0.62 instead of 1.0.
